# Recommendation network on one core: the order of weight splits, feature copies and loads in the start phase and in layer 2 of the first tile, and the last tile border

## What is computed

```python
fm = emb_table[jnp.arange(N_CAT)[None, :], cat_idx]          # 512 x 26 x 128
h = jax.nn.relu(dense_x @ Wd1 + bd1)
h = jax.nn.relu(h @ Wd2 + bd2)
dense = jax.nn.relu(h @ Wdf + bdf)                           # 512 x 128
Z = jnp.concatenate([fm, dense[:, None, :]], axis=1)
S = jnp.einsum('bie,bje->bij', Z, Z)
iu, ju = np.triu_indices(N_CAT + 1, k=1)
x = jnp.concatenate([S[:, iu, ju], dense], axis=-1)          # 351 pairs + 128
x = jax.nn.relu(x @ Wt1 + bt1)                               # 1024
x = jax.nn.relu(x @ Wt2 + bt2)                               # 1024
x = jax.nn.relu(x @ Wt3 + bt3)                               # 512
x = jax.nn.relu(x @ Wt4 + bt4)                               # 256
return jax.nn.sigmoid(x @ Wo + bo)
```

## Time and profile before

| | |
|---|---|
| median of 3 runs | 184.23 us (183.07 to 185.62) |
| the profiled execution | 183.0 us, of which 181.2 us is the span in the profile |
| PE busy | 162.3 us (90%) |
| DVE, ACT, POOL busy | 72.5, 63.2 and 100.4 us |
| granted clock of PE | 1.00 throughout |
| transfers | 18.18 MB, mean 100 GB/s |

### The profile page before, as it was taken

How to read it: one execution, slowest core, us unless ns; L and a number is a source line. 1 busy time by engine, 2 the same in 40 slices (tenths; PEclk the granted TensorE clock), 3 DMA queues, 4 the chain that set the end, 5 groups by cost and what they waited for, 6 DMA issues and landing times.

```text
span 181.2 us, 3886 instructions
## 1 busy us (share of the span) xinstructions
PE 162.3 (90%) x1693; PEld 115.7 (64%) x1693; DVE 72.5 (40%) x135; ACT 63.2 (35%) x108; POOL 100.4 (55%) x111
## 2 busy tenths in 40 slices
PE   2999996658899499989999999799999988999993
PEld 1334453325577378767778787587878766788981
DVE  5004367665745467262422135335032145422311
ACT  3375787386227855221212022221111212201110
POOL 4777777777777777777777777777750000000000
PEclk9999999999999999999999999999999999999999
DMA  3999999249865221221212212212220000000000
GB/s 60 314 367 257 257 312 364 83 113 321 301 180 163 60 58 33 62 58 47 58 46 59 58 47 62 52 50 58 48 61 0 0 4 0 0 4 0 0 0 0
DMA packets 6674, 18.18 MB, mean 100 GB/s; under 512 B 2309, under 2 KB 2441, under 8 KB 6530
## 3 DMA queue, kind: packets, MB, share of 16 engines
q1 hardware_dynamic: 3330, 11.12, 19.4%
q0 software_dynamic: 3328, 6.82, 14.2%
HBM read 17.93 MB, written 0.00 MB: 99 GB/s over the span
## 4 chain that ended last, share of the span: by engine, by line
PE 68%; POOL 10%; DVE 7%; ACT 5%; issue 5%; DMA 4%; DVEq 0%
PE mp L475 25%; POOL rows L335 10%; PE mp L498 10%; PE mp L442 9%; PE gp L400 6%; PE tp L450 5%; PE gp L390 5%; PE mp L539 3%; DMA rows<-in_emb,row_of 3%; PE gp L516 3%; DVE xb L775 2%; ACT tp L613 2%; DVE w2l L747 1%; PE gp L412 1%; ACT xth L635 1%
## 5 line engine op out<-in xcount | busy, mean ns | idle before, releaser
L335 POOL DMA_INDIRECT rows<-in_emb,row_of x104 | 99.5, 957 | 33.2 <-issue 29.3
L475 PE MATMUL mp<-w2h,a1h 128*128 128x512 f32 x64 | 26.3, 411 | 2.5 <-DVE w3l L747 2.5
L475 PE MATMUL mp<-w2l,a1h 128*128 128x512 f32 x64 | 26.8, 418 | 0.0
L475 PE MATMUL mp<-w2h,a1l 128*128 128x512 f32 x64 | 25.5, 399 | 0.0
L624 ACT COPY zt<-gp 128x512 f32<-128x512 f32 x16 | 9.4, 586 | 30.1 <-PE gp L390 30.0
L390 PE MATMUL gp<-ident,rows 128*128 128x128 f32 x104 | 16.6, 274 | 3.0 <-DMA rows<-in_emb,row_of 3.0
L390 PEld LDWEIGHTS gp<-ident,rows 128*128 128x128 f32 x104 | 13.0, 141 | 9.2 <-DMA rows<-in_emb,row_of 3.9
L400 PEld LDWEIGHTS gp<-zt 128*32 128x32 f32 x1024 | 11.2, 110 | 7.3 <-issue 6.7
L475 PEld LDWEIGHTS mp<-w2h,a1h 128*128 128x128 f32 x64 | 12.1, 188 | 5.3 <-DVE w3l L747 2.9
L797 DVE TENSOR_TENSOR raw<-mp,bc 128x512 f32<-128x512 f32 x8 | 5.5, 691 | 24.3 <-PE mp L475 24.3
L747 DVE TENSOR_TENSOR w2l<-w,tp 128x1024 fp32r<-128x1024 f32 x7 | 8.5, 1220 | 14.9 <-ACT tp L613 14.9
(11 more groups left out here) (82 smaller groups left out, 247.4 us busy)
## 6 DMA issues: line engine op xcount, KB each, us to landing
w<-in_wt SPq DMA_DIRECT2D x13, 512.0 KB, 6.2
rows<-in_emb,row_of POOLq DMA_INDIRECT x104, 2.7
w<-in_wt SPq DMA_DIRECT2D x3, 468.0 KB
bc<-in_rows SPq DMA_DIRECT2D x1, 1024.0 KB, 6.2
wd_sb<-in_wd SPq DMA_DIRECT2D x1, 512.0 KB, 3.6
w1d<-in_wt SPq DMA_DIRECT2D x1, 512.0 KB, 7.1
bt<-in_rows SPq DMA_DIRECT2D x1, 512.0 KB, 10.4
wdf_sb<-in_wdf SPq DMA_DIRECT2D x1, 128.0 KB, 3.1
```

The source lines that it names most:

```text
L335: pool.indirect_dma_start(out=rows[:, n % RING, :], out_offset=None, in_=emb.rearrange("c v e -> (c v) e"), in_offset=bass.IndirectOffsetO ...
L475: last = pe.matmul(mp[:, h, :], a[:, k, :], w[:, k, cols], start=(k == 0 and part == 0), stop=(k == M1 - 1 and part == 2))
```

## The change

It moves instructions on ACT, DVE and PE, cuts the high parts of pieces 10 to 17 differently, and has SP keep three loads under way. Nothing is computed that was not computed before.

- `IN_FLIGHT` is 3.
- On DVE, the low parts of pieces 3 and 5 stand ahead of the copies of groups 3 and 5; `dense_products_out(7)` stands ahead of group 7, the low part of piece 8 after the transposed sums.
- On ACT, group 4 stands ahead of piece 5 and group 6 ahead of piece 8. Piece 9's high part stands ahead of the pair copies, its middle part after them. The high part and the middle part are functions of their own; high parts are made for a whole load (1024 columns) at a time, also for w2's last block and for w3.
- In layer 2 of tile 0, pieces 10 to 13 use bank 1 and 14 to 17 bank 0. Piece 10 is split ahead of the second half of a1 on both engines.
- On PE, `dense_products(7)` follows number 6 directly, and one of the `keep_warm` products of 512 columns is gone.
- Layer 4 stands after 5 products of the next layer 1, not after 4. The border between tiles 2 and 3 has the order of the other two.

```diff
-FEATURES_3 = [{1: [5], 8: [6], 12: [7]}] * 2 + [{4: [5], 14: [6]}, {}]
+FEATURES_3 = [{1: [5], 8: [6], 12: [7]}] * 3 + [{}]
-GRAMS_3 = [{5: 2, 15: 3}] * 2 + [{10: 2}, {}]
-LATE = TILES - 2
-LAYER_4_IN_1 = 4
+GRAMS_3 = [{5: 2, 15: 3}] * 3 + [{}]
+LAYER_4_IN_1 = 5
...
-IN_FLIGHT = 4
+IN_FLIGHT = 3
...
-SPLITS_H0, SPLITS_H1 = WHOLE_SPLITS + 5, WHOLE_SPLITS + 8
+SPLITS_H0, SPLITS_H1 = WHOLE_SPLITS + 4, WHOLE_SPLITS + 8
...
             dense_products(6)
+            dense_products(7)
             pe.wait_ge(pre_out, 7)
             keep_warm(512)
+            transpose_features(0, 6)
+            keep_warm(256)
+            transpose_features(0, 7)
+            grams(0, 3)
             keep_warm(512)
-            transpose_features(0, 6)
-            keep_warm(512)
-            transpose_features(0, 7)
-            keep_warm(256)
-            grams(0, 3)
-            dense_products(7)
             keep_warm(512)
             transpose_pairs(0)
...
-            for t in range(LATE):
+            for t in range(TILES - 1):
                 layer_1(t)
                 layer_2(t)
                 layer_3(t)
                 transpose_pairs(t + 1)
-            t = LATE
-            layer_1(t)
-            layer_2(t)
-            layer_3(t)
-            transpose_features(t + 1, 7)
-            turn(t, 4)
-            grams(t + 1, 3)
-            layer_4(t)
-            transpose_pairs(t + 1)
...
+            def high_part(n):
+                name, k = LOADS[n]
+                if name == "w1":
+                    weights, high = w1[0:PC, k, :], w1h[0:PC, k, :]
+                elif name == "w2":
+                    weights, high = w2[:, k, :], w2h[:, k, :]
+                else:
+                    weights, high = [w[:, k:k + 2, :].rearrange("p k n -> p (k n)") for w in (w3, w3h)]
+                sc.wait_ge(w_in[n], 16)
+                sc.copy(high, weights).then_inc(w_hi, 1)
+            def middle_part(n):
+                at_least(sc, w_lo, n)
+                if n == WHOLE_SPLITS:
+                    sc.wait_ge(raw_ready, 2)
+                if n == SPLITS_H0:
+                    sc.wait_ge(raw_ready, 3)
+                sc.copy(split_bank(n).bitcast(F32R), split_weights(n)[0]).then_inc(w_mid, 1)
```

More of the change, by code:

```diff
@@ L428, in layer_1 @@
                         pe.wait_ge(xt_lo, t + 1)
-                    if n == 2 and 0 < t <= LATE:
+                    if n == 2 and t > 0:
                         turn(t - 1, 4)
-                    if n == LAYER_4_IN_1 and 0 < t <= LATE:
+                    if n == LAYER_4_IN_1 and t > 0:
                         layer_4(t - 1)
@@ L600, in _ @@
         def _(sc):
-            def split_hi(n):
[L602 to L613, removed]
+            def high_part(n):
[15 more added lines that the diff above has]
+                sc.copy(split_bank(n).bitcast(F32R), split_weights(n)[0]).then_inc(w_mid, 1)
+            def split_hi(n):
+                high_part(n)
+                middle_part(n)
             def bottom_out(n):
@@ L668, in _ @@
             split_hi(4)
+            features(0, 4)
             split_hi(5)
-            features(0, 4)
             split_hi(6)
             split_hi(7)
+            features(0, 6)
             split_hi(8)
-            features(0, 6)
-            split_hi(9)
+            high_part(9)
             pairs_out(0)
+            middle_part(9)
             for t in range(TILES - 1):
@@ L682, in _ @@
                 layer_1_hi(t, 0)
+                if t == 0:
+                    high_part(WHOLE_SPLITS)
+                    middle_part(WHOLE_SPLITS)
                 for n in range(PRODUCTS_2):
@@ L686, in _ @@
                         if t == 0:
-                            for k in range(WHOLE_SPLITS, SPLITS_H0 - 2):
-                                split_hi(k)
+                            middle_part(WHOLE_SPLITS + 1)
+                            high_part(LOADS_12)
+                            middle_part(WHOLE_SPLITS + 2)
+                            middle_part(WHOLE_SPLITS + 3)
                     for g in FEATURES_2[t].get(n, ()):
@@ L692, in _ @@
                     if n == PRODUCTS_2 // 2 - 1 and t == 0:
-                        for k in range(SPLITS_H0 - 2, SPLITS_H0 + 1):
-                            split_hi(k)
+                        high_part(LOADS_12 + 1)
+                        middle_part(SPLITS_H0)
                     if n == TURN_2:
@@ L697, in _ @@
                         if t == 0:
-                            for k in range(SPLITS_H0 + 1, len(SPLITS)):
-                                split_hi(k)
+                            middle_part(SPLITS_H0 + 1)
+                            high_part(LOADS_12 + 2)
+                            middle_part(SPLITS_H0 + 2)
+                            middle_part(SPLITS_H0 + 3)
+                            high_part(LOADS_12 + 3)
                 for n in range(PRODUCTS_3):
@@ L705, in _ @@
                         layer_2_hi(t, 1)
[L706 to L709, removed]
-                    relu_3(t)
-                    pairs_out(t + 1)
+                pairs_out(t + 1)
+                relu_3(t)
             t = TILES - 1
@@ L822, in _ @@
             dense_products_out(1)
+            split_lo(3)
             features(0, 3)
-            split_lo(3)
             dense_products_out(2)
@@ L834, in _ @@
             split_lo(7)
-            split_lo(8)
+            dense_products_out(7)
             features(0, 7)
             turn_sums(0)
-            dense_products_out(7)
+            split_lo(8)
             pairs_lo(0)
@@ L851, in _ @@
                     if n == TURN_1B:
+                        if t == 0:
+                            split_lo(WHOLE_SPLITS)
                         layer_1_lo(t, 1)
                         if t == 0:
-                            for k in range(WHOLE_SPLITS, SPLITS_H0):
+                            for k in range(WHOLE_SPLITS + 1, SPLITS_H0):
                                 split_lo(k)
@@ L875, in _ @@
                         layer_2_lo(t, 1)
[L876 to L886 removed]
+                turn_sums(t + 1)
+                layer_3_sum(t)
+                pairs_lo(t + 1)
+                last_layers(t)
             t = TILES - 1
```

20 lines of the change are left out of this document (3 added, 17 removed).

## The result

The change takes 177.17 us, the median of 4 runs (176.75 to 179.07), against 183.77 for the kernel before; the ratio is 0.964, with an interval from 0.955 to 0.973. The forecast was 177.0, with a range from 175.0 to 180.8.

A forecast was written before the change was run, and what follows sets the result against it. PE bound by the start phase's ladder and a wait in layer 2 of tile 0. Terms 3.6 + 2.6 - 0.4 + 0.2 + 0.2 + 0.4 = 6.6, cut to 6.5: 176.5 from 183.0, 177.7 from the median; said 177.0, range 175.0 to 180.8.

The forecast's parts named there:

- The start phase: Before layer 1 of tile 0: new order and three loads bring group 7's copy forward, 3.1 to 4.1 us, taken as 3.6.
- the ladder: Start phase: ACT and DVE pass one shared bank to and fro, 2.3 us a piece; layer 1 waits for it, it for gather 19.
- the rival with the late gather at the head of ACT: Start phase: group 4's copy ahead of piece 5 lets gather 16's lateness delay the ladder; 2.5 us later gives 179.0; chance 0.13.
- lower bound of 3.1: Start phase: gain in us if gathers land as before, group 7 copied at 39.4 instead of 42.46.
- Loads in flight: Start phase: with three loads instead of four, gather 19 lands up to 1.4 us sooner; gain 3.1 up to 4.1.
- Layer 2 of tile 0: PE's wait for w3's low parts ahead of the second half goes, as bank 1 is free at 59.6: 2.6 us.
- DVE's queue behind the pieces: Tile 0 after layer 2: piece 18's low part delays DVE's sum and group 5's copies: -0.4 us, ends 0 and -0.8.
- The borders: First two tile borders: one more product of 0.23 us fills PE's 0.31 us wait ahead of layer 4: +0.2 each.
- The last border: Border of tiles 2 and 3: loses the 0.6 us wait on `raw`, gets the others' layer 4 wait: +0.4, ends 0 and 0.6.
- The cut by the gathers: Tile 2's last gather, in at 103.6, lets PE gain at most 5.9 of 6.0 us up to there: cut 0.1.
- The wait in layer 2: Rival, tile 0: w_lo late or layer 3 waits for 18; half of 2.6 us gone, 178.5 to 179.5; chance 0.14.
- a late load 9: Rival "Slower": layer 1 waits for load 9, wanted at 41.2; beyond 47.7 the whole 6.5 us gain is gone; chance 0.03.

The follow-up runs named there:

- e11: The change with w3's last low part later on DVE, w3's loads one behind the other, and two loads in flight instead of three: 177.12 us (176.82 to 177.45).
- e1: The change once more, unaltered, for another profiled execution: 177.06 us (176.76 to 178.6), ratio 0.966.
- e3: The kernel before with the start phase's new order alone, four loads in flight: 181.03 us (179.41 to 182.82), ratio 0.985.
- e8: The change with two loads in flight instead of three: 176.89 us (176.83 to 177.41), ratio 0.965.
- e9: The change with the low part of w3's last piece moved behind group 5's copies on DVE: 177.17 us (176.01 to 177.66).
- e10: The change with w3's loads one behind the other, bias rows together with the last, instead of two at a time: 176.74 us (176.03 to 179.02).
- e2: The change with four loads in flight instead of three: median 177.80 us of five executions (177.08 to 178.01); a sixth took 225.25.
- e6: The change with two idle products of 512 columns on PE ahead of group 5's transposes: 177.47 us (176.84 to 178.19).
- e12: The change with w3's last low part later on DVE and w3's loads one behind the other, three loads in flight: 177.2 us (176.3 to 179.1).
- second profile: The profiled execution of e1, the unaltered change run again: 177.13 us, span 175.3.
- e4: The kernel before with the new pieces and high parts of layer 2 alone: 181.73 us (179.93 to 183.61), ratio 0.986.
- e7: The kernel before with idle products, two ahead of group 5 and two ahead of the wait for the `dense` sums: 184.14 us (183.17 to 185.63), ratio 1.004.
- e5: The kernel before with the last border like the others and layer 4 behind five products, alone: 182.51 us (181.36 to 185.47), ratio 0.993.

## Why the prediction was right, point by point

**The start phase: the ladder as forecast, its head misread, the total in part luck.** 3.6 was said and 3.56 measured. From group 5's copy to group 7's the working has 5.5 us (33.88 to 39.4). In the nine profiles with this order and a clock of 1.00 up to layer 1 it took 5.5 to 5.8 us, but for e11 (6.5, with a wait of 0.71 us for a gather ahead of group 6). So the two engines do pass the bank as worked out.

What starts the ladder is another matter. The working lets it follow gather 19, and takes half of what a sooner landing could give. In e1, e3, e8, e9 and e10, however, DVE took up group 5's copy without idle time, straight behind piece 5's low part, which hangs on group 4's copy and so on gather 16. That is the path of the rival with the late gather at the head of ACT. From e1 to e8 group 4's transposes come 0.70 us sooner (28.55 against 29.25) and group 5's copy 0.71 us sooner (32.98 against 33.69), while gather 19 lands 1.30 us sooner after its issue (4.17 against 5.47). Only in e2, e6, e11 and e12 did DVE wait for group 5 (0.91, 0.60, 0.20 and 0.69 us). The working's own numbers say as much: piece 5's low part ends at 33.6 there, so a sooner gather 19 alone could give 0.3 us, and not the 1.0 between 3.1 and 4.1.

In e1 group 7's copy stands 3.07 us sooner, which is the working's lower bound of 3.1. The other 0.48 us came between this copy and the transposed sums (1.44 us instead of 1.92), a stretch that the working took as unchanged. In the profiles with this order it takes 1.36 to 1.89 us, and no run shows why. From the sums to layer 1 it is 3.24 to 3.26 us in all of them. So the mechanism is right from group 5 on, and that 3.56 came so near to 3.6 is luck. Gather 19 and the gain still go together (landings of 6.42, 5.47, 5.41 and 4.17 us in e2, e1, e3 and e8, gains of 2.39, 3.56, 3.55 and 4.51 us), but in three of these four it was not what DVE waited for. In the longest profile (179.07) it was: gather 19 took 6.75 us, DVE was idle for 1.67 us ahead of group 5's copy, 2.2 us of gain are left by the working's rule, and the rest of the loss is the clock, below.

**Loads in flight: an effect on gather 19, and one load is hardly more than the scatter.** From gather 19's issue to group 5's transposes it took 4.4 to 6.5 us in six profiles with four loads (median 5.9), 4.8 to 6.8 in six with three (median 5.5), and 4.2 and 3.9 in two with two. So two loads lie below all others, and between four and three the profiles cannot tell; the 0.7 to 0.9 us between e2 and the change speak for three. The text had 0 to 1.0 us for the fourth load and took half. Gather 32 tells more: 2.8 to 3.6 us with one transfer of SP's at a time, 5.8 to 7.2 us with a load and the bias rows beside it. The rule of the Trainium skill (page "DMA: Bandwidth & Descriptors", section "Queues, rings and completion order"), by which each DMA engine takes turns between its queues packet by packet, would have had no effect of how many loads stand in SP's queue. The two profiles with two loads and the landings of gather 32 do not agree with that; gather 19's landings beside three and four loads do not decide it.

**Layer 2 of tile 0: right, 2.6 said, 2.31 in the second profile.** The hole is gone in every kernel with the four pieces; e4, without an earlier start, shows 2.76, and the profile of 179.07 2.93. What is missing in the second profile is no fault of the pieces: group 1 of tile 1 waited for gather 32, and e10, with fewer transfers beside that gather, has 15.49, the value of e4.

**DVE's queue behind the pieces: mechanism right, size off.** -0.4 was said with -0.8 as its end, -0.89 measured (-0.86 in e4). The step put the delay on piece 18's low part, and that is the instruction that the trace shows: 1024 columns at 64.81, right ahead of the sum and group 5's copies. The sum starts 0.66 us behind layer 3's start, and started 0.20 behind it before. Moving the low part gives 0.57 back, and e9's wait of 0.25 us for a gather hides some more (estimate: 0.8 of the 0.89). PE's own wait for the copies was only 0.22 us; the working left out that the runs of short products behind it would be longer too, and why they are stays open.

**The borders: right in place, but 0.2 each was no gain in the end.** The wait ahead of layer 4 is down to 0.07 us at tile 1, and layer 1 of tiles 1 and 2 gained 0.24 and 0.23. But layer 2 of these tiles is 0.2 longer; product by product, 0.19 of it lies on one run of 64 short products for the first quarter (0.93 us instead of 0.76 in tile 1), whose work the change does not alter. This is no scatter: layer 2 takes 15.50 to 15.55 us in both tiles in all profiles with the change's three parts, and 15.31 to 15.35 in the kernel before, e3, e4 and e7. The border alone (e5) has 15.33 in tile 1 and 15.55 in tile 2. So at least in tile 2 the 0.2 comes with the new order of the border; its cause stays open.

**The last border: place right, +0.4 said, +0.84 measured.** The wait on `raw` of 0.57 is gone as said. The step took the work as equal. It is not: PE is busy for 16.48 us in the new stretch and for 16.81 in the old one, where quarter, layer 4 and pairs stood one behind the other with no product of layer 3 among them; that this order is the reason was not tried. That is 0.33, and 0.57 + 0.33 less some 0.1 more of waits ahead of layer 1 and layer 4 is the 0.8. The windows over the stretch, before and then in the second profile (sum of the span, busy time of each engine):

```profile
sum 18.00, PE 16.81 PEld 13.02 DVE 7.43 ACT 3.97 POOL 0.00; mean PE 8.41 PEld 6.51 DVE 3.71 ACT 1.99 POOL 0.00
```

```profile
sum 17.14, PE 16.48 PEld 12.81 DVE 7.52 ACT 3.98 POOL 0.00; mean PE 8.24 PEld 6.40 DVE 3.76 ACT 1.99 POOL 0.00
```

**The cut by the gathers: there, but at another gather and too small.** The text looked at tile 2's last gather, with a landing of 2.6 us, and took 0.1. In the second profile that gather was in at 102.39, 2.2 us ahead of its group. The first to cut is gather 32, issued at 43.56 while a load and the bias rows were under way: it needs 6.8 us, not 2.6, and its group's place in the change is just that early. The next one is gather 51, in at 70.78 where its group starts at 70.83. The mis-step was to take the landing from a quiet stretch for a loaded one, where the earlier trace rows had the right size. It cost 0.3 to 0.5 in the sum (0.27 of it at the group itself); but it means that in this profile the ladder, which most of the working was about, no longer set the end once it was 3.6 us shorter.

**The sum and the baseline.** 6.5 was worked out and 5.86 measured between the two profiles: layer 2 of tile 0 gave 0.3 less than said, DVE's queue cost 0.5 more, the later layers 2 took back 0.4, and the last border gave 0.4 more. From the profiled 183.0 that makes 177.1. That the median also came out at 177.1, from a median of 183.8 to 184.2 before, is owed to something that the text had not worked out: the kernel before ran in most of its runs at a granted clock of 0.991 or less (181.7 to 183.3 us at 1.00, 183.1 to 185.6 at 0.991), the change in most of its runs at 0.995 to 1.00. One stretch of 3.41 us at 0.50, as e4 and e5 show it, makes a mean of 0.991 over a span of 181 us (estimate: 1 - 1.7/181). In e4 and e5 it stands at the start phase's gap ahead of the idle products, which the change does away with. Clocks of 0.991 or less were in 9 of 11 runs of the kernel before beside e1 to e4, in 4 of 6 of e3, which keeps the gap in layer 2, in 3 of 6 of e4, which keeps those of the start phase, and in 2 of 6 of the change. So both places may have a share; the runs are too few to say how much, and idle products in e7 did not help.

**Signs listed ahead.** Group 7's copy was due at 38.4 to 39.4 and stood at 39.39, layer 1 at 43.5 to 44.6 and stood at 44.08; no wait on w3l; gather 19 in at 32.8, between the two values named; PE waiting for gathers in layer 2 of tile 0, not in layer 3. Two signs listed as against showed as well. A granted clock below 1.00 was in both profiles: in the longer one behind the gap ahead of group 5, in the second (0.997) only from 174.29 us on, behind a wait of 0.98 us ahead of the last products. And ACT stood idle for 2.48 us ahead of group 4's copy in the other; the low part of piece 5 still began at 32.55, ahead of gather 19's landing at 32.80. So the rival with a late gather at the head of ACT came in its path, since this low part and not gather 19 then set group 5's copy, but without the 2.5 us that it priced. The wait in layer 2 did not come, nor a late load 9: it was in at 33.65 in the change and at 32.78 with two loads, and ACT took it up at 41.23.

## What to carry to other kernels

When a ladder of two engines is shortened, look anew for the operand that comes last at its new head; here it was group 4's copy and no longer gather 19. Then follow every stream that was not sped up, gather by gather, from the first one on whose issue and landing meet the new places, with landing times from a stretch that carries as many loads; the end of a tile is not the first place where they meet. An instruction that only fills a bank or a late operand goes behind the short copies and sums for which PE waits, not ahead of them. And before small edits are added up, look whether the chain that ended last still goes over them: after this change five kernels that each took 0.5 to 1.5 us out ahead of the floor moved the time by nothing that could be told from the scatter.

## What was not expected of the hardware

**The clock behind a gap.** In the profile of 179.07 us PE's granted clock fell in the start phase (PE busy, weights, DVE, ACT, POOL, then PE's clock, share and rate of transfers):

```profile
31.00:34.00 3.00, 0.35 (x1) 0.00 (x0) 2.13 (x3) 2.69 (x4) 2.22 (x3) 0.97 0.45 163
34.00:36.00 2.00, 1.78 (x5) 1.03 (x5) 0.62 (x2) 1.51 (x2) 1.55 (x2) 0.50 0.27 70
36.00:38.00 2.00, 2.00 (x66) 1.15 (x66) 1.14 (x2) 0.00 (x0) 1.53 (x2) 0.70 0.28 70
```

PE stood still for 2.87 us ahead of group 5 (34.22), and from 33.79 on it was at 0.50, the lower of its two levels (1.2 GHz), for 3.4 us; from group 5 to layer 1 it took 12.5 us instead of 11.2. The same was seen in e4 (from 38.47, at the end of a gap of 1.94 us) and in e5 (from 38.22, 1.0 us behind a gap of 1.93), both ahead of idle products. But a gap of 2.12 us at 38.59 in the kernel before, one of 2.47 in e2 and the four of 2.47 us in layer 2 (before, e3, e5 and e7) were followed by a clock of 1.00. So a gap of that size may cost 1.2 us or nothing.

**POOL's late issues.** In nine of the fourteen profiles one gather's issue took 1.4 to 2.0 us instead of 0.944, at 65 to 70 us, within 2.0 us of the first product of layer 3 of tile 0; in e1, e3, e6, e9 and e10 none near it did. Before, PE had 6 us to spare at tile 1's last gather; in e12 the hitch made that gather 0.96 us later, and PE waited for it. What makes it was not tried.

**Runs of 64 short products.** A quarter's products took from 0.75 to 0.99 us with equal shapes, in different places in different kernels. That too stays open.
